# Results of the experts stored in token order, so that their readers need no gather

## The reference

```python
probs = jax.nn.softmax(xt @ w_router, axis=-1)
top_w, top_i = jax.lax.top_k(probs, TOP_K)          # 4 of 16 experts
top_w = top_w / jnp.sum(top_w, axis=-1, keepdims=True)
cw = jnp.zeros((T, E)).at[jnp.arange(T)[:, None], top_i].add(top_w)
g = silu(einsum('td,edh->teh', xt, we1)) * einsum('td,edh->teh', xt, we3)
moe_out = jnp.einsum('teh,ehd->td', g * cw[:, :, None], we2)
shared = silu(xt @ ws1) * (xt @ ws3) @ ws2
out = shared / (k + 1) + moe_out * (k / (k + 1))
```

## Time and profile before

| what | value |
|---|---|
| median of 3 runs | 2773.62 us (2769.53 to 2778.78) |
| span of the profiled execution, its own time | 2889.1 us |
| mean granted TensorE clock in it | 0.925 |
| TensorE busy | 2486.6 us, 86% |
| VectorE busy | 1963.1 us, 68% |
| ScalarE busy | 1445.2 us, 50% |
| GpSimd busy | 1097.0 us, 38% |
| DMA, GpSimd's queue | 38400 packets, 104.91 MB |

### The profile page before, as it was taken

The page is one execution under the profiler, slowest core; times in us unless marked ns, Lnnn a source line. Parts: engine busy times, 40 slices in busy tenths (PEclk is TensorE's granted clock), DMA queues, the critical chain, the costliest instruction groups (busy, mean ns, idle before and its releaser), DMA issues. The chain is left out here.

```text
span 2889.1 us, 49366 instructions
## 1 busy us (share of the span) xinstructions
PE 2486.6 (86%) x15174; PEld 1604.9 (56%) x15190; DVE 1963.1 (68%) x5524; ACT 1445.2 (50%) x3366; POOL 1097.0 (38%) x1556
## 2 busy tenths in 40 slices
PE   7885997788799999968868994899679999996998
PEld 5664996455333333446648993677553333334776
DVE  6654887665688888656646884665568887875444
ACT  3332554232287877723324552333546887874443
POOL 5663444776322222335653446662132222220000
PEclk9997998898799999978989996999788999998999
DMA  3435555555534464343345554331473354434000
GB/s 119 150 123 145 179 179 174 157 165 171 130 85 92 95 128 93 85 159 124 126 131 170 178 178 148 98 107 48 143 178 68 78 116 99 99 96 154 30 32 27
DMA packets 251508, 350.78 MB, mean 121 GB/s; under 512 B 42437, under 2 KB 200694, under 8 KB 245110
## 3 DMA queue, kind: packets, MB, share of 16 engines
q1 hardware_dynamic: 212854, 242.71, 32.2%
q0 software_dynamic: 38400, 104.91, 10.3%
HBM read 196.80 MB, written 149.92 MB: 120 GB/s over the span
## 5 line engine op out<-in xcount | busy, mean ns | idle before, releaser
L1299 DVE CUSTOM_DVE_ANT_0 attn_heads_masked_s<-attn_heads_s_ps,attn_heads_causal 128x768 bf16<-128x768 f32 (+7 forms) x1024 | 726.7, 754 | 143.6 <-PE attn_heads_s_ps L1101 126.6
L1218 ACT ACTIVATE attn_heads_probs<-attn_heads_st_ps 128x512 f32<-128x512 f32 (+3 forms) x1536 | 663.4, 495 | 234.1 <-PE attn_heads_st_ps L1120 220.2
L1609 POOL DMA_INDIRECT xs_dram<-moe_route_xn,rows_at x256 | 262.0, 1023 | 182.3 <-DVE rows_at L1877 110.4
L1136 PE MATMUL attn_heads_o_ps<-attn_heads_probs,attn_v_sb 128*32 128x512 f32 (+3 forms) x3072 | 329.1, 501 | 2.1 <-POOL attn_heads_probs L1043 1.9
L1043 POOL TENSOR_SCALAR_AFFINE_SELECT attn_heads_probs<-attn_heads_probs 128x512 f32<-128x512 f32 x256 | 163.0, 637 | 364.5 <-ACT attn_heads_probs L1218 359.3
L1120 PE MATMUL attn_heads_st_ps<-attn_heads_more_st 99*128 99x512 bf16 x960 | 261.7, 330 | 0.1
L1101 PE MATMUL attn_heads_s_ps<-attn_heads_more_st 96*128 96x512 bf16 (+1 forms) x960 | 246.7, 335 | 9.8 <-DMA attn_heads_more_st<-k_dram 4.8
L2105 POOL DMA_DIRECT2D ys_dram<-moe_expert_y_sb x288 | 157.3, 546 | 244.7 <-DVE moe_expert_y_sb L2223 244.2
L1120 PEld LDWEIGHTS attn_heads_st_ps<-attn_heads_more_st 99*128 99x128 bf16 x960 | 84.5, 97 | 212.7 <-ACT attn_heads_probs L1218 159.7
L2137 PE MATMUL moe_expert_gu_ps<-moe_w_hi,moe_expert_xT_hi 128*128 x576 | 189.4, 329 | 0.9 <-DVE moe_expert_xT_lo L2205 0.7
L1101 PE MATMUL attn_heads_s_ps<-attn_stack 96*128 96x512 bf16 (+2 forms) x576 | 157.6, 358 | 27.6 <-DVE attn_heads_row_max L1299 11.3
(11 more groups left out here) (276 smaller groups left out, 6137.0 us busy)
## 6 DMA issues: line engine op xcount, KB each, us to landing
moe_expert_x_sb<-xs_dram SPq DMA_DIRECT2D x288, 128.0 KB, 2.1
ys_dram<-moe_expert_y_sb POOLq DMA_DIRECT2D x288, 128.0 KB, 2.1
o_dram<-attn_heads_oT SPq DMA_DIRECT2D x64, 256.0 KB, 5.7
moe_route_w_raw<-in_L_ffn_we_dram SPq DMA_DIRECT2D x96, 128.0 KB
q_dram<-attn_proj_parts SPq DMA_DIRECT2D x32, 384.0 KB, 2.8
k_dram<-attn_proj_parts SPq DMA_DIRECT2D x32, 384.0 KB, 2.7
x_mid<-moe_route_x_sb SPq DMA_DIRECT2D x16, 512.0 KB
attn_v_sb<-o_dram SPq DMA_DIRECT2D x32, 256.0 KB
```

What stands on the lines that cost most here:

```text
L1136: last = pe.matmul(o_ps[h * VW:(h + 1) * VW, use % OB, TILE - w:TILE], v_sb[:, at:at + VW], probs[:, G % NR, h, 0:w], start=(j == 0), stop ...
L1218: act.activation(probs[:, G % NR, h, 0:w], st_ps[:, v % NB, 0:w], ACT.Exp, scale=scale)\
L1299: dve.tensor_tensor_reduce(out=masked_s[:, use % 4, 0:w], in0=s_banks[:, at * TILE:at * TILE + w], in1=causal[:, SEQ - w:SEQ], scale=1.0, ...
L1609: pool.indirect_dma_start(xs_dram, bass.IndirectOffsetOnAxis(rows_at[:, n * SUB + s, k:k + 1], 0), xn[:, n % RX, s, :], None).then_inc(sca ...
```

## The change

- The results' array `y_dram` has a row for each token and choice, token by token. In the expert stage GpSimd's plain store becomes an indirect one that scatters a slot's 128 rows there.
- The row number travels with the row: a row of `xs_dram` has 16 more floats, one per expert. VectorE computes them in `find_rows_y`, by counting how many of the experts before one were chosen. In the expert stage ScalarE picks the column of the slot's expert, by a register that it loads from DRAM every four slots, and turns it into integers (`take_rows`).
- The spare region grows to 2048 rows, whose row numbers lead to rows that nobody reads. A second DMA writes these numbers from `spare_y`, which shares memory with `match`; so `locate(0)` waits for it. Pads carry such numbers too.
- Readers load four rows of each of 128 tokens by one plain DMA. `rstd_of` comes ahead of all loads of the next tile.
- `rows_at` is not rewritten; `find_slots` has two operations fewer. Some tensors of the route share memory now (`left` with `shifted`, `cw_raw` with `logit`).

```diff
@@ -74,6 +74,9 @@
+
+DX = D + E
+ROWS_Y = TOK * TOP_K
@@ -88,21 +91,20 @@
-def gather_rows(pool, u, y_sb, y_used, y_loaded, ys_dram, rows_at):
+def load_rows_y(pool, u, y_sb, y_used, y_loaded, y_dram):
...
-    for k in range(TOP_K):
-        pool.indirect_dma_start(y_sb[:, r, k, :], None, ys_dram, bass.IndirectOffsetOnAxis(rows_at[:, u, k:k + 1], 0))\
-            .then_inc(y_loaded[r], 16)
+    rows = y_dram[u * P * TOP_K:(u + 1) * P * TOP_K, :].rearrange("(p k) d -> p k d", k=TOP_K)
+    pool.dma_start(y_sb[:, r, :, :], rows).then_inc(y_loaded[r], 16)
...
-        dve.wait_ge(y_loaded[(u + s) % ring], 64 * ((u + s) // ring + 1))
+        dve.wait_ge(y_loaded[(u + s) % ring], 16 * ((u + s) // ring + 1))
@@ -186,7 +188,7 @@
         if combine:
-            x_out, ys_dram, rows_at, cw_at, y_loaded = combine
+            x_out, y_dram, cw_at, y_loaded = combine
@@ -343,18 +345,16 @@
                 def gather(u):
-                    gather_rows(pool, u, y_sb, y_used, y_loaded, ys_dram, rows_at)
+                    load_rows_y(pool, u, y_sb, y_used, y_loaded, y_dram)
...
-                    if combine and t + 1 < TILES:
-                        gather((t + 1) * SUB)
...
-                        for s in range(1, SUB):
+                        for s in range(SUB):
@@ -1435,11 +1435,14 @@
         region_top = sb("region_top", [P, E])
-        zeros = sb("zeros", [P, D])
+        zeros = sb("zeros", [P, DX])
+        before_e = sb("before_e", [P, 2, SUB, E + E // 2], BF16)
+        first_y = sb("first_y", [P, SUB])
+        spare_y = match[:, :, :, :].rearrange("p s k e -> p (s k) e")
...
-        upto = sb("upto", [P, E, E])
+        upto = sb("upto", [P, E, E], BF16)
@@ -1561,8 +1565,10 @@
                 before.clear(sp)
-                sp.wait_ge(consts_ready, 1)
-                sp.dma_start(xs_dram[SPARE:SPARE + P, :], zeros[:, :]).then_inc(spare_zeroed, 16)
+                sp.wait_ge(consts_ready, 3)
+                spare = xs_dram[SPARE:SPARE + E * P, :].rearrange("(j p) d -> p j d", p=P)
+                sp.dma_start(spare[:, :, 0:D], zeros[:, 0:D].unsqueeze(1).to_broadcast([P, E, D])).then_inc(spare_zeroed, 16)
+                sp.dma_start(spare[:, :, D:DX], spare_y).then_inc(spare_zeroed, 16)
@@ -1588,7 +1594,7 @@
                 sp.wait_ge(slots_stored, 32)
-                sp.wait_ge(spare_zeroed, 16)
+                sp.wait_ge(spare_zeroed, 32)
@@ -1604,13 +1610,21 @@
                     pool.wait_ge(rows_ready, n + 1)
+                    pool.wait_ge(ahead_step, 5 * (n + 1))
...
-                pool.memset(zeros[:, :], 0.0).then_inc(consts_ready, 1)
+                pool.memset(zeros[:, 0:D], 0.0).then_inc(consts_ready, 1)
+                pool.iota(zeros[:, D:DX], pattern=[[P, E]], base=ROWS_Y, channel_multiplier=1,
+                          allow_small_or_imprecise_dtypes=True).then_inc(consts_ready, 1)
+                pool.iota(spare_y[:, :, :], pattern=[[P, E], [0, E]], base=ROWS_Y + E * P, channel_multiplier=1,
+                          allow_small_or_imprecise_dtypes=True).then_inc(consts_ready, 1)
+                pool.memset(before_e[:, :, :, 0:E // 2], 0.0).then_inc(consts_ready, 1)
+                pool.iota(first_y[:, :], pattern=[[P * TOP_K, SUB]], base=-1, channel_multiplier=TOP_K,
+                          allow_small_or_imprecise_dtypes=True).then_inc(consts_ready, 1)
@@ -1857,6 +1871,24 @@
+                def find_rows_y(n):
+
+                    pad = E // 2
+                    counted = chosen[:, n % 2, :, :]
+                    b = before_e[:, :, :, :]
+                    dve.wait_ge(xn_ready, n + 1)
+                    dve.tensor_copy(b[:, 0, :, pad:], counted).then_inc(ahead_step, 1)
+                    for step, back in enumerate((1, 2, 4)):
+                        dve.wait_ge(ahead_step, 5 * n + step + 1)
+                        dve.tensor_tensor(b[:, (step + 1) % 2, :, pad:], b[:, step % 2, :, pad:], b[:, step % 2, :, pad - back:pad - back + E],
+                                          ALU.add).then_inc(ahead_step, 1)
+                    dve.wait_ge(ahead_step, 5 * n + 4)
+                    dve.tensor_tensor(b[:, 0, :, pad:], b[:, 1, :, pad:], b[:, 1, :, 0:E], ALU.add).then_inc(cum_ready, 1)
+                    dve.wait_ge(cum_ready, n + 1)
+                    dve.scalar_tensor_tensor(out=xn[:, n % RX, :, D:DX], in0=b[:, 0, :, pad:], scalar=float(n * TILE * TOP_K),
+                                             in1=first_y[:, :].unsqueeze(2).to_broadcast([P, SUB, E]), op0=ALU.add, op1=ALU.add)\
+                       .then_inc(ahead_step, 1)
@@ -1876,6 +1908,8 @@
                        .then_inc(rows_ready, 1)
+                    if n == 0:
+                        dve.wait_ge(spare_zeroed, 32)
@@ -1915,20 +1949,17 @@
                     dve.tensor_reduce(slot_from[:, :], ended_at[:, :, :], AX.X, ALU.max).then_inc(slot_step, 1)
-                    dve.tensor_scalar(slot_used[:, :], slot_e[:, :], E - 0.5, None, ALU.is_lt).then_inc(slot_step, 1)
...
+                    dve.wait_ge(slot_step, step + 11)
+
+                    dve.tensor_scalar(slot_off[:, :], slot_e[:, :], float(REGION), float(-SPARE), ALU.mult, ALU.add).then_inc(slot_step, 1)
...
-                    dve.tensor_scalar(slot_off[:, :], slot_e[:, :], float(REGION), float(-SPARE), ALU.mult, ALU.add).then_inc(slot_step, 1)
-                    dve.wait_ge(slot_step, step + 13)
...
-                    dve.wait_ge(slot_step, step + 14)
-                    dve.tensor_tensor(slot_from[:, :], slot_row[:, :], slot_used[:, :], ALU.mult).then_inc(slot_step, 1)
-                    dve.wait_ge(slot_step, step + 15)
-                    dve.tensor_scalar(slot_tab[:, 1, :], slot_from[:, :], float(SPARE), None, ALU.add).then_inc(slots_ready, 1)
+                    dve.wait_ge(slot_step, step + 13)
+                    dve.tensor_scalar(slot_tab[:, 1, :], slot_row[:, :], float(SPARE), None, ALU.add).then_inc(slots_ready, 1)
@@ -1971,10 +2002,11 @@
                 dve.wait_ge(pads_ready, 1)
-                dve.wait_ge(consts_ready, 9)
+                dve.wait_ge(consts_ready, 13)
...
+                find_rows_y(0)
@@ -2001,6 +2033,7 @@
                             choose(t + 1)
+                            find_rows_y(t + 1)
@@ -2077,37 +2107,21 @@
                         _, rows = nc.values_load_multi_w_load_instructions(
-                            slot_dram[1:2, s:s + BATCHED], engines=[SP_ENGINE], min_val=0, max_val=SPARE,
+                            slot_dram[1:2, s:s + BATCHED], engines=[SP_ENGINE], min_val=0, max_val=SPARE + (E - 1) * P,
...
+                        sp.wait_ge(rows_ready, s - AHEAD + 1)
...
-                def move_rows(e):
-
-                    pool.wait_ge(rows_step, 2 * e)
-                    pool.tensor_scalar(moved[:, :], rows_x[:, :], float(e * REGION), gap[:, e - 1:e], ALU.is_ge, ALU.mult)\
-                        .then_inc(moved_step, 1)
-                    pool.wait_ge(moved_step, e + 1)
-                    pool.tensor_tensor(rows_y[:, :], rows_y[:, :], moved[:, :], ALU.add).then_inc(rows_step, 2)
-
-                at = rows_at[:, :, :].rearrange("p u k -> p (u k)")
-                pool.tensor_copy(rows_x[:, :], at).then_inc(rows_step, 1)
-                pool.tensor_scalar(gap[:, :], tiles[:, :], float(P), float(-REGION), ALU.mult, ALU.add).then_inc(rows_step, 1)
-                pool.wait_ge(rows_step, 2)
-                pool.tensor_copy(rows_y[:, :], rows_x[:, :]).then_inc(moved_step, 1)
-                pool.wait_ge(moved_step, 1)
...
-                    pool.dma_start(ys_dram[s * P:(s + 1) * P, :], y_sb[:, s % AHEAD, :]).then_inc(y_stored[s % AHEAD], 16)
-                    if s % 8 == 0 and 1 <= s // 8 < E:
-                        move_rows(s // 8)
-                pool.wait_ge(rows_step, 2 * E)
-                pool.tensor_copy(at, rows_y[:, :]).then_inc(rows_step, 1)
-                pool.wait_ge(rows_step, 2 * E + 1)
+                    pool.wait_ge(rows_ready, s + 1)
+                    pool.indirect_dma_start(y_dram, bass.IndirectOffsetOnAxis(rows_y[:, s % RI:s % RI + 1], 0), y_sb[:, s % AHEAD, :], None)\
+                        .then_inc(y_stored[s % AHEAD], 16)
@@ -2190,9 +2204,24 @@
+                def take_rows(s):
+
+                    if s >= RI:
+                        act.wait_ge(y_stored[s % AHEAD], 16 * ((s - RI) // AHEAD + 1))
+                    act.activation(rows_y[:, s % RI:s % RI + 1], x_sb[:, s % AHEAD, D:DX][:, bass.ds(expert[s], 1)], ACT.Copy)\
+                        .then_inc(rows_ready, 1)
+
+                expert = {}
                 for i in range(SLOTS + 2):
+                    if i % BATCHED == 0 and i < SLOTS:
+                        _, found = nc.values_load_multi_w_load_instructions(
+                            slot_dram[0:1, i:i + BATCHED], engines=[ACT_ENGINE], min_val=0, max_val=E - 1,
+                            skip_runtime_bounds_check_because=why)
```

(57 more changed lines are left out.)

## The result

| | median | runs |
|---|---|---|
| before | 2773.3 us | 2769.53 to 2778.78 |
| after | 2749.39 us | 2747.28 to 2751.12 |

The ratio is 0.990, 95% interval 0.9876 to 0.9923: 24 us faster, where I forecast 6 slower, and outside my range.

What follows compares the result with a forecast made beforehand. TensorE, busy 86%, was taken as the bound; -29.6 (readers) -1 +5 +2.6 +15 (row numbers) +14 (spare rows) gave +6.0 us on 2773.62, predicted 2779; own range 2772 to 2787, of all 2756 to 2805.

Steps and rivals of the forecast that it cites:

- What bounds the kernel now: Whole kernel: TensorE busy 86% of the span, time won only where it waits or a stage's chain is late.
- The readers' gain: Projection and table phases: one load for four gathers and earlier 1/std save 15.1 and 14.5 us, together 29.6.
- What the scatter of results costs: Expert stage: indirect stores cost GpSimd 0, ScalarE's load of expert numbers +5 us, the stages' ends +2.6.
- GpSimd's term of 0: Expert stage: an indirect store takes 1.26 us a slot against 1.47, so GpSimd keeps up at no cost.
- ScalarE's load, +5: Expert stage: ScalarE's load of four expert numbers every four slots takes 0.52 us, 0.07 of it exposed: +5 us.
- +2.6 for the ends: Ends of the expert stages: the last store is 0.42 us longer and lands later, +1.3 us each.
- My upper bound by GpSimd, 37 us: Expert stage: at 1.6 us an indirect store GpSimd would set the pace, 0.13 us x 288 = 37 us.
- What finding the row numbers costs: Routing: find_rows_y adds 1.5 us of VectorE a tile, 1.07 of it delaying TensorE's h_lo: 14 tiles, +15 us.
- What the spare rows cost: Heads of both routes: VectorE stalls 5.3 and 5.9 us for the clearing; with find_rows_y(0), +14 us.
- Rival B: Routing: row numbers hidden but for 5 us, spare rows 3 us a head: -12 us, 2762; chance 30%.
- the 3.95 us for the table phase's second tile: Table phase: part of its 14.5 us gain, beside 7 at the head and 3.5 for later tiles.
- 4 x 1.4: Projection phase: four of eight tiles have 1/std late; issuing it ahead of all loads saves 5.7 us.

Runs made afterwards that it cites:

- a_late4: The changed kernel with the spare rows' numbers in yT's memory, so VectorE waits at the end of tile 0: 2738 us, ratio 0.9842 to before's 2782.
- b_clean4: The kernel before, unchanged, run again for a profile on a chip where before takes 2782 us: 2784 us.
- a_late: The changed kernel with the spare rows' numbers in yT's memory, on a chip where before takes 2879 us: 2945 us, ratio 1.0227.
- a_plain2: The changed kernel with plain stores in slot order instead of indirect ones in the expert stages: 2844 us, ratio 0.9868 to before's 2881.

## Why the prediction was wrong

- **What bounds the kernel now.** "GpSimd is nowhere the busiest engine" misled in the projection phase. I took its busy share and left out the 0.30 us of issue, which I had in the earlier trace rows and used for the expert stage. A tile's 16 gathers at 1.12+0.30 us and the 1/std chain's 1.5 are 24 us of the 25.6 to 27.9 that a tile had.
- **The readers' gain.** Table phase: 14.5 predicted, 14.7 measured (279.1 to 264.4), its mechanism right in part: TensorE's wait of 38.8 us at the head fell to 33.9, 5 us where I had taken 7, and the tiles with the 4.58 us of the second gave 10 where I had taken 7.5 (six of their seven distances were 27.8 to 31.6 us; in after five are 27.4 to 27.5). That the sum came out is luck. Projection phase: 15.1 predicted, 25 measured. I summed waits (3, 6.4 and 5.7) where the pace of a nearly full engine was the cost. The late 1/std, to which I gave 5.7 and a place in the change's merit, is worth nothing by order alone.
- **What the scatter of results costs.** GpSimd's term of 0 was right on kind A, to 2 ns an instruction. ScalarE's load, +5: nothing is seen (235 to 237 us both), and +2.6 for the ends neither. My upper bound by GpSimd, 37 us, is the price of a pace of 1.6 us; an instruction of 1.6 us, as the prediction has it, would with its 0.30 of issue cost (1.9-1.47) x 288 = 124. On kind B the stages lose 58 us each, with the instruction at 0.96 us, by a mechanism that no rival of mine had. The Trainium skill's rule on the shared port pair ("SBUF — State Buffer", Who interferes with whom) agrees with the trace: with VectorE 83% busy, each operation with an operand from PSUM, not one store of the 288 was longer than 976 ns.
- **What finding the row numbers costs: +15. This is the step that failed.** Measured on kind A: 0 within 3 us by medians, with the counting done twice, and routings no longer than before's once the head stalls are gone (a_late4). The step took the wait of 13.4 us for h_lo to lie on the path of every tile. That wait was a mark of the condition and not of the kernel: TensorE was the bound of routing (94 to 95% busy), with VectorE at 78%.
- **What the spare rows cost.** 5.3 and 5.9 us of stall predicted, 4.66 and 4.58 measured; two heads 14, and the routings are 3 to 5 and 6 to 7 us longer, a_late4 wins back 7 to 12. Right, somewhat large: find_rows_y(0) adds little. In the DMA packets of after's trace a 64-byte piece took 11 ns of a DMA engine in the first head and 8 in the second, a 1 KB piece 46: all 2048 took 1.5 and 1.3 us of the 16 engines, as I had estimated, and not 6.5. The Trainium skill's rule on transfers under 512 B ("DMA: Bandwidth & Descriptors", Specifications) agrees with the trace in the rate, 64 B in 11 ns against 1024 B in 46; the price that I had read from it did not hold here.

The sum: +6 less 15 (row numbers), 7.6 (ScalarE and ends), 10 (projection) and some 4 (heads of routes) is -31; measured -24 to -30. Rival B had the right sign, half of the size and the first of its two reasons. Three more figures do not come out: the 3.95 us for the table phase's second tile has no source (the wait was 4.58), 4 x 1.4 is 5.6, and by the rivals' own shares the chances are 0.25 faster, 0.33 within and 0.42 slower.

I had the warning: the profiled execution was 4% longer than the timed runs, and I scaled all by 4% instead of asking which stages carried it. By the stage ends of that profile and of b_clean4 they were the routings (250.3 for 210.2 us, 261.5 for 212.9) and the projection (267.9 for 250.4), the very stages in which I read waits.

## What to carry to other kernels

When the profiled execution is some per cent longer than the timed runs, find the stages that carry the difference before a wait in them prices a step; a wait that only that execution has is no room and no path. Occupancy of an engine that issues DMAs is its busy time and the issue gaps between: near the tile's length it has a part in the pace, and then summed waits price it too low (25 us for 15 here), and a new order can lose (38 us here). Try a change on more than one chip: this one is 1.0 to 1.2% faster on one kind and, by its near copies, 1.7 to 2.6% slower on the other.

## What the runs showed that I had not expected

- Two kinds of chips for the same kernel, 2773 to 2782 and 2871 to 2881 us, with the same heads of the first attention (493 to 497 us) and the same granted clock in the expert stage (1.00). The difference lies in stages with indirect DMAs of GpSimd: in three profiles of before 40 to 44 and 38 to 49 us in the routings, 15 to 18 in the projection, 2 to 4 in the table phase. Without their gathers the projection takes 224 us and the table phase 263 on kind B (a_late), as in after on kind A, and a_plain2 shows the same for the stores of the expert stage. For the routings no run shows what carries it.
- On kind B one indirect store a slot makes an expert stage 294 us long in place of 236, and plain stores from the same engine cost nothing.
- A clearing of 2.1 MB and 2048 pieces of 64 B, waited for in a head, held VectorE for 4.6 us; on kind A it costs nothing to be seen if the wait stands some 27 us later, at the end of tile 0.
